# The tail of an attention and expert kernel: work after the attention ordered by a list scheduler

## What is computed

```
x = layernorm(x + attention(x))     # 16 heads of 16 channels, rotary, causal softmax; head i's scores get
                                    # cascade_w[i-1] * mean over the queries of head i-1's probabilities
x = layernorm(x + experts(x))       # 8 experts, each token goes to the one with the largest logit
    sel = argmax(x @ gate_w.T);  rw = sigmoid(max(x @ gate_w.T))
    xs = x * rw;  out = (xs @ w_up[sel].T * silu(xs @ w_gate[sel].T)) @ w_down[sel].T
layernorm(x) = (x - mean) / sqrt(var + 1e-5)
```

## Time and profile before

| | |
|---|---|
| median of three runs | 3644.92 us |
| lowest and highest | 3643.49, 3656.99 us |
| profiled execution: span | 3649.0 us |
| its busy shares: TensorE, VectorE, ScalarE, GpSimd | 86%, 72%, 85%, 55% |
| end of the attention (last attention instruction on VectorE) | 3398 us |
| routing's count, first gather of group 3, last scatter | 3486.0, 3518.2, 3645.4 us |

### The profile page before, as it was taken

The page is one execution under the profiler, slowest core; times in us unless marked ns, Lnnn a source line. Parts: engine busy times, 40 slices in busy tenths (PEclk is TensorE's granted clock), DMA queues, the critical chain, the costliest instruction groups (busy, mean ns, idle before and its releaser), DMA issues. The chain is left out here.

```text
span 3649.0 us, 92468 instructions
## 1 busy us (share of the span) xinstructions
PE 3133.0 (86%) x29690; PEld 1595.9 (44%) x29690; DVE 2612.1 (72%) x7930; ACT 3097.2 (85%) x8898; POOL 2009.9 (55%) x6184
## 2 busy tenths in 40 slices
PE   5788888888999889989998888899998888888855
PEld 3333333333444434444444443444444443344645
DVE  7566666666777777877877778787787767777666
ACT  3799999999998988988888999889888899988324
POOL 5555555554555356765665455675665633445345
PEclk8899999999999999999999999999999999999968
DMA  4332323333433443444444333435534432345354
GB/s 158 96 71 63 80 57 73 80 76 82 99 83 83 115 99 97 121 112 117 109 107 107 101 76 82 117 105 139 141 84 102 100 81 61 71 108 153 110 179 165
DMA packets 222519, 370.65 MB, mean 102 GB/s; under 512 B 49941, under 2 KB 165405, under 8 KB 209936
## 3 DMA queue, kind: packets, MB, share of 16 engines
q1 hardware_dynamic: 205968, 323.19, 35.9%
q0 software_dynamic: 14976, 37.34, 3.8%
q10 hardware_dynamic: 1088, 4.19, 0.3%
HBM read 259.76 MB, written 104.40 MB: 100 GB/s over the span
## 5 line engine op out<-in xcount | busy, mean ns | idle before, releaser
L1047 DVE CUSTOM_DVE_ANT_0 att_a<-scores,window 128x128 f32<-128x128 f32 (+7 forms) x2048 | 1508.6, 754 | 802.4 <-PE scores L720 654.4
L905 ACT ACTIVATE att_a<-att_a,neg_max 128x128 f32<-128x128 f32 (+7 forms) x2048 | 1598.0, 780 | 116.6 <-DVE neg_max L1047 112.9
L917 ACT ACTIVATE att_t<-scores 128x1024 f32<-128x1024 f32 (+7 forms) x2048 | 1334.6, 652 | 176.4 <-PE scores L739 163.5
L737 PE MATMUL scores<-q_stack,k_stack 104*128 104x512 bf16 (+3 forms) x3072 | 821.7, 335 | 328.6 <-ACT att_t L917 139.3
L755 PE MATMUL pv<-att_t,v_sb 128*32 128x256 f32 (+7 forms) x16384 | 828.7, 297 | 8.7 <-DVE o_sb L1081 8.2
L720 PE MATMUL scores<-k_stack,q_stack 99*128 99x512 bf16 (+3 forms) x3072 | 734.5, 334 | 28.1 <-DVE att_t L1094 10.1
L1389 POOL TENSOR_SCALAR guess<-row_sum 128x8 f32<-128x8 int32 x256 | 55.4, 216 | 1134.9 <-ACT att_a L905 1133.9
L755 PEld LDWEIGHTS pv<-att_t,v_sb 128*32 128x32 f32 x16384 | 376.5, 109 | 515.9 <-issue 428.3
L737 PEld LDWEIGHTS scores<-q_stack,k_stack 104*128 104x128 bf16 x3072 | 240.2, 98 | 735.4 <-DVE neg_max L1047 362.4
L739 PE MATMUL scores<-identb,mask 128*128 128x128 bf16 x2048 | 456.0, 223 | 0.0
L917 ACT ACTIVATION_READ_ACCUMULATOR att_t<-scores 128x1 f32 x2048 | 427.5, 209 | 0.0
(11 more groups left out here) (350 smaller groups left out, 4191.5 us busy)
## 6 DMA issues: line engine op xcount, KB each, us to landing
runner_r<-in_experts SPq DMA_DIRECT2D x137, 384.0 KB, 4.1
qk_parts<-of_proj SPq DMA_DIRECT2D x128, 384.0 KB, 2.6
q_stack<-qk_parts SPq DMA_DIRECT2D x378, 128.0 KB
k_stack<-qk_parts SPq DMA_DIRECT2D x378, 128.0 KB
of_proj<-in_xt SPq DMA_DIRECT2D x28, 1024.0 KB, 5.4
head_out<-o_sb SPq DMA_DIRECT2D x252, 64.0 KB
x_rows<-finisher_f SPq DMA_DIRECT2D x26, 514.0 KB, 4.7
finisher_f<-head_out SPq DMA_DIRECT2D x52, 256.0 KB, 5.1
```

What stands on the lines that cost most here:

```text
L737: engine.matmul(scores[:, c0:c1], ks[0:ROWS_B, j * P:(j + 1) * P], qs[0:ROWS_B, j * P + c0 - base:j * P + c1 - base], start=True, stop=True)
L905: engine.activation(taken, taken, EXP, scale=-1.0, bias=neg_max[:, n, i:i + 1], accum_out=row_sum[:, n, i:i + 1]).then_inc(s_exp_a, 1)
L917: engine.activation(att_t[:, ring:ring + end - base], scores[:, base:end], EXP, accum_out=col_sum[:, n, j:j + 1]).then_inc(s_exp_b, 1)
L1047: engine.tensor_tensor_reduce(out=att_a[:, ring:ring + end - base], in0=scores[:, base:end], in1=window[:, T - (end - base):T], op0=ALU.ad ...
```

## The change

All behind the attention, the steps are no longer made by `step(None, None)` but by a new function `by_readiness()`. It plays the tail on five engines with a table of durations, `EFFORT` (us of work, and us until a DMA's data have landed; all engines and all data free at time 0). Each time it looks for the stage with the earliest start, and on that stage's engine it takes, among the stages that could start within 0.2 us of it, first finishing and routing, then the lower group, then the earlier start. Each such stage becomes a step of its own. Second, group 3's batches get `t_root` on GpSimd and one Newton step on VectorE like all others. Third, `t_scale`, `t_turned` and `t_norm` are on ScalarE wherever they fall into the tail, not only in group 3 (`t >= TAIL` in place of `n[0] == GROUPS - 1`, with a wait in ScalarE for VectorE's last one before, `early`). `MIDWAY` only renames which stages carry on their job's bank. Nothing ahead of the tail changes.

```diff
     def norm_job(g, of):
-        root = [Stage("t_root", b, 2, phase=GPSIMD), Stage("t_newton", b, LAG)] if g < GROUPS - 1 else [Stage("t_newton", b, 1)]
-        return ([Stage("t_aggr", b, 0, after=tuple(("t_stat", (g, j), 1) for j in of))] + root + [Stage("t_norm", b, 1)]
+        return ([Stage("t_aggr", b, 0, after=tuple(("t_stat", (g, j), 1) for j in of)),
+                 Stage("t_root", b, 2, phase=GPSIMD), Stage("t_newton", b, LAG), Stage("t_norm", b, 1)]
...
+    BROUGHT = {"f_add": "f_x", "t_scale": "t_gather", "t_gu": "t_weights"}
+    HANDOVER = 0.1
+    PATIENCE = 0.2
+    EFFORT = dict(
+        f_load=Effort("SP", 0.2, 5.0), f_x=Effort("SP", 0.1, 5.0), f_pa=Effort("PE", 0.85), f_pb=Effort("PE", 0.85),
+        f_add=Effort("DVE", 1.5), f_aggr=Effort("DVE", 1.0), f_root=Effort("POOL", 1.0), f_newton=Effort("DVE", 0.9),
+        f_norm=Effort("ACT", 2.1), f_t=Effort("PE", 0.75), f_tm=Effort("ACT", 0.6),
...
+        t_gather=Effort("POOL", 1.0, 3.0), t_weights=Effort("SP", 0.4, 5.0), t_scale=Effort("ACT", 0.5),
+        t_turn=Effort("PE", 0.45), t_turned=Effort("ACT", 0.38), t_gu=Effort("PE", 1.1),
+        t_tanh=Effort("ACT", 0.3), t_gate=Effort("DVE", 0.28), t_up=Effort("DVE", 0.28), t_down=Effort("PE", 0.6),
+        t_add=Effort("DVE", 0.42), t_stat=Effort("DVE", 0.42), t_aggr=Effort("DVE", 0.8), t_root=Effort("POOL", 0.9),
+        t_newton=Effort("DVE", 0.9), t_norm=Effort("ACT", 0.6), t_out=Effort("POOL", 1.0, 3.0))
...
+            def rank(job):
+                s = job[0]
+                if s.kind[:2] in ("f_", "r_"):
+                    return 0
+                return s.key[0]
+            while active:
+                starts = [(earliest(job), n) for n, job in enumerate(active)]
+                starts = [(at, n) for at, n in starts if at is not None and at < float("inf")]
+                first, n = min(starts)
+                engine = EFFORT[active[n][0].kind].engine
+                _, at, n = min((rank(active[n]), at, n) for at, n in starts
+                               if at <= first + PATIENCE and EFFORT[active[n][0].kind].engine == engine)
...
-        while active:
-            step(None, None)
+        by_readiness()
...
-                    elif kind == "t_norm" and n[0] == GROUPS - 1:
+                    elif kind == "t_norm" and t >= TAIL:
+                        act.wait_ge(s["t_norm"], early["t_norm"])
...
                     elif kind == "t_newton":
-                        if n[0] < GROUPS - 1:
-                            dve.wait_ge(s["t_root"], nth["t_root", n])
-                            newton_step(norm_of(n), 1, s["t_newton"], False)
-                        else:
-
-                            y_ = norm_of(n).newton[:, 1, :].bitcast(I32)
-                            dve.wait_ge(s["t_aggr"], nth["t_aggr", n])
-                            dve.wait_ge(s_dve, chained(engine.tensor_scalar(y_, y_, -0.5, float(0x5f3759df), ALU.mult, ALU.add)))
-                            newton_step(norm_of(n), 3, s["t_newton"], True)
+                        dve.wait_ge(s["t_root"], nth["t_root", n])
+                        newton_step(norm_of(n), s["t_newton"], ("t_norm", n) in late)
```

More of the change, by code:

```diff
@@ L318, in step @@
                         banks[s.bank], used_by[s.bank] = t + 1, (s.kind, s.key)
-                    elif s.kind.endswith("_b") and id(job) in held_by:
-                        s.bank = held_by[id(job)]
-                    elif s.kind in ("f_pb", "r_sum", "t_tanh", "t_gate") and not s.hold:
+                    elif s.kind in MIDWAY and not s.hold and id(job) in held_by:
                         s.bank = held_by[id(job)]
@@ L419, in block_kernel @@
     steps, nth, total, PROLOGUE, TAIL = timetable()
+    late = {(st_.kind, st_.key) for step_ in steps[TAIL:] for st_ in step_.stages if st_.kind in ("t_scale", "t_turned", "t_norm")}
+    early = {kind: total[kind] - len([k for k, _ in late if k == kind]) for kind in ("t_scale", "t_turned", "t_norm")}
     TILE_OF = {(g, j): (j % RUN[g], j // RUN[g]) for g in range(GROUPS) for j in range(TILES)}
@@ L975, in scalar_program @@
                         made.then_inc(s["t_norm"], 1)
-                    elif kind == "t_turned" and n[0] == GROUPS - 1:
+                    elif kind == "t_turned" and t >= TAIL:
+                        act.wait_ge(s["t_turned"], early["t_turned"])
                         was = earlier(n)
@@ L981, in scalar_program @@
                         engine.copy(runner_of(n).xwT, room[:, 0:C]).then_inc(s["t_turned"], 1)
-                    elif kind == "t_scale" and n[0] == GROUPS - 1:
+                    elif kind == "t_scale" and t >= TAIL:
+                        act.wait_ge(s["t_scale"], early["t_scale"])
                         r, (b, _), was = runner_of(n), XS[n], earlier(n)
@@ L1009, in half, with newton_step @@
                 engine.tensor_scalar(norm.newton[:, 2, :], norm.moments[:, :, 1], EPS, -0.5, ALU.add, ALU.mult).then_inc(sem, 1)
-            def newton_step(norm, times, sem, shift):
+            def newton_step(norm, sem, shift):
                 a_, y_, h_ = (norm.newton[:, k, :] for k in range(3))
[L1014 to L1022, removed]
+                ev = chained(engine.tensor_tensor(a_, y_, y_, ALU.mult))
+                dve.wait_ge(s_dve, ev)
+                ev = chained(engine.tensor_tensor(a_, a_, h_, ALU.mult))
+                dve.wait_ge(s_dve, ev)
+                made = engine.scalar_tensor_tensor(out=norm.rstd, in0=a_, scalar=1.5, in1=y_, op0=ALU.add, op1=ALU.mult)
                 if shift:
+                    dve.wait_ge(s_dve, chained(made))
                     made = engine.scalar_tensor_tensor(out=a_, in0=norm.moments[:, :, 0], scalar=-1.0, in1=norm.rstd, op0=ALU.mult,
@@ L1351, in vector_program @@
                         chained(engine.bn_stats(norm_of(b).stats[:, b[1].index(n[1]), :], y_of(n)))
-                    elif kind == "t_norm" and n[0] < GROUPS - 1:
+                    elif kind == "t_norm" and t < TAIL:
                         norm = norm_of(n)
```

58 lines of the change are left out of this document (55 added, 3 removed).

## The result

The changed kernel takes 3633.24 us, median of six runs (3630.31 to 3635.83), beside 3648.32 us for the kernel before in the same session. The ratio is 0.9945 with a 95% interval of [0.993, 0.9959]: faster by 0.4 to 0.7%, about 20 us by the ratio, where 50 were forecast (3595 us, range 3574 to 3622). The two medians lie 15.1 us apart and the two profiled executions 20.5. The profiled execution took 3630.31 us with a span of 3628.5.

What follows compares the result with a forecast made beforehand. Step order was taken to bound finishing, VectorE's chain routing, and GpSimd then the rounds group 3's tiles, with GpSimd bounding them after the change. Savings of 34 + 7 + 9 = 50 us off 3644.9 gave 3595 us, range 3574 to 3622.

Steps and rivals of the forecast that it cites:

- A: Finishing, from 3400 us to `r_count`: bound by step order, 86 us to become 52, 34 us less.
- B: Routing, from `r_count` to group 3's first gather: VectorE's chain, 32.2 us to become 25, 7 less.
- C: Group 3's tiles, first gather to last scatter's end: GpSimd becomes the bound, 128.1 us to become 119, 9 less.
- 5.1 us, or 41 too: TensorE's price in finishing: 5.1 us a quad for projections, transposes and gates, 41 us for eight quads.
- What stands in GpSimd's queue of group 2: Group 2's leftover GpSimd work in group 3's stretch: an estimated four scatters, 5 us.
- an estimated 5 us of waiting: At the end, after GpSimd's last gather: waiting for a batch's aggregate, root, Newton step and norm, 5 us.
- The roots at their full 10 us: Group 3's ten roots moved to GpSimd, about 1.0 us each, would cost its tiles' stretch 10 us.
- TensorE's clock: Rival: thinly spread work keeps TensorE's clock low in group 3's tiles, 12 us longer there, 3616 us; chance 0.10.
- Waiting roots: Rival: roots stand before gathers in GpSimd's queue, group 3's tiles take 138 us, total 3614 us; chance 0.10.
- DMA at nothing: Changed order of SyncE's loads and stores in group 3's tiles costed at nothing, DMA share under 0.7.
- Group 2 last: Rival: group 2's tiles finish last, runners 0 to 3 start 25 us late, about half lost, 3622 us; chance 0.08.
- Slower: Rival: estimated durations misplace GpSimd's root and scatter groups, waits at each batch; at 8 us each 3665 us; chance 0.04.

Runs made afterwards that it cites:

- e5: Changed kernel with the scheduler's 40 durations replaced by measured ones; ratio to the kernel before 0.9934.
- e7: Changed kernel with one more four-column `pow` on GpSimd ahead of each of group 3's 39 gathers; ratio to the kernel before 1.0024.
- e9: Changed kernel without group 2's scatters behind group 3's first gather, their output rows not written; ratio to the kernel before 0.989.
- e2: Changed kernel with group 3's roots back on VectorE (guess and three Newton steps); ratio to the kernel before 0.9929.
- e1: Changed kernel with the old order of steps, keeping roots on GpSimd and the tail's stages on ScalarE; ratio to the kernel before 1.0001.
- e8: Changed kernel with measured durations, scheduler patience 0 in place of 0.2, and group 3's roots back on VectorE; ratio to the kernel before 0.9882.
- e11: Changed kernel with measured durations and scheduler patience 0 in place of 0.2, roots on GpSimd; ratio to the kernel before 0.9886.
- e3: Changed kernel with `t_scale`, `t_turned` and `t_norm` of group 2's tail tiles back on VectorE; ratio to the kernel before 0.9945.

## Why the prediction was wrong

The sign holds, and so does the mechanism in A and B and GpSimd as C's bound. The size doesn't: of the 41 us expected in A and B 31.2 came, and C, which was to give 9, took 11.0 back. By its steps:

**A, 34 us: the right cause, sized too high.** Quad after quad goes through, and ScalarE's norms are spread instead of standing in a block:

```profile
3419.13 2.08 ACT L1054 ACTIVATE finisher_f<-finisher_f 128x256 f32<-128x256 f32 x4 [4.74 <-DVE finisher_f L1112]
3423.07 2.07 ACT L1054 ACTIVATE of_proj<-of_proj 128x256 f32<-128x256 f32 x4
3429.35 2.08 ACT L1054 ACTIVATE of_proj<-of_proj 128x256 f32<-128x256 f32 x4 [1.53 <-DVE of_proj L1112]
...
3450.53 2.07 ACT L1054 ACTIVATE k_stack<-k_stack 128x256 f32<-128x256 f32 x4
```

`r_count` came 25.9 us earlier. The term that fell short is TensorE's: "5.1 us, or 41 too" for finishing and "4 for group 2's stages that get in". It was busy for 54.0 of A's 60 us. By line and in sum, finishing's matmuls show 47.3 us and those of group 2's tiles 13.3, 6.6 of them overlapping each other. The projection's price, 0.22 a record, was taken from one run at full speed; in A 112 of its 128 records (the others come ahead of 3400) took 28.4 us, 0.25 each, and transposes and gates 18.9 in place of 12.8. That TensorE sets A's length is shown by the executions of one order at two clocks above. The prediction costed the clock in A at nothing, though its own row had 0.85 there; between a clock of 0.90 and one of 0.95 it is 2.6 us. A sum of 60 was within the stated bounds of 43 and 65. Part of it is the plan: e5, with better durations, is 4.1 us earlier than e7.

**B, 7 us: right**, 5.3 measured. VectorE is busy for 25.1 of 28 us there, but for 46.1 of 60 in A, so the prediction's check, which let it be near full in both, holds for B alone. Routing's last result is there at 3484.1; the 3 us up to the gather are two scatters of group 2 on GpSimd.

**C, 9 us less: wrong by 20.** Two terms of it failed. "What stands in GpSimd's queue of group 2 (an estimated four scatters, 5 us)" was 20.0 us: 11 scatters, a gather, five roots. Four scatters came from no row. The earlier trace rows showed VectorE adding a tile of group 2 as late as 3502.75 even in the old order, and the change puts finishing and routing ahead of group 2 for all of A and B; four scatters were too few by the prediction's own reasoning. It named the place in B ("group 2's remaining tiles now fall here") and then did not carry their scatters into the stretch that it had just called bound by GpSimd. e7 shows that bound directly (38.1 us for 39.8), e9 the scatters' share in it (10.2 of 14.1 us). The second term, "an estimated 5 us of waiting" at the end, was 10.1: after its last gather GpSimd waits for ScalarE four times (2.61, 4.27, 2.86 and 1.58 us, of which 0.30 each are the usual gap), each time shortly behind a root whose Newton step and norm must come first. It has 25 scatters there and not some 20, but they are in the 98.7 all the same. 98.7 + 10.3 + 20.0 + 10.1 are C's 139.1. (The prediction's 108.9 for DMAs and roots should read 108.7; it changes nothing.)

**The roots at their full 10 us: right for this kernel, not as a rule.** C loses 8.4 us to them here (e2), 0.8 in the old order (e1) and 0.6 in the best (e8 and e11).

**The third part: no gain or loss that the runs can tell from nothing** (e3), but not by the working given: taking some 15 us off VectorE did not shorten A and B, which are shorter with the stages on VectorE, and that gain is paid back in late work.

**The signs.** `r_count` at 3460.1 lies 1.1 us outside 3452 ± 7, and the first gather at 3487.0 outside 3477 ± 8. Up to 3580 GpSimd is busy for over 0.75, as said; from 3580 to 3629 it is 0.59, and not only in the last 10 us.

**Rivals.** TensorE's clock did not fall in C as a whole; up to 3580 it was 0.90, where it had been 0.77 up to 3600, as the engine was busier (65.3 of 92 us against 56.7 of 82). Behind that it was 0.67, and whether this lengthens the last waits no run shows. The Trainium skill (TensorE: Matmul & The Clock Gate, A second HAM failure mode: psum-queue depth-cycling) tells of short idle times that make the clock swing. In C up to the last gather that can't have cost anything, as GpSimd never waits. In A, where the prediction did not look for it, the clock fell behind idle times of 0.78 and 1.27 us in one execution and not in another, and cost 2.6 to 4.8 us. Idle times alone, then, do not decide it here.

Waiting roots: no wait of over 3 us in the midst of C; the one of 4.27 and its three neighbours at the end are of this kind, 5 us more than the sum had for them. DMA at nothing: up to the last gather GpSimd waits for no data either, though the DMA share was 0.71 up to 3580, a little over the 0.7 that was said.

Group 2 last: the nearest in cause, and priced wrongly. With the plan's order laid beside the trace's gathers, runners 0 to 3 start group 3 at 3487.04, 3500.07, 3508.88 and 3528.19, runners 4 to 7 at 3488.34, 3506.38, 3507.63 and 3517.88. On average both sets start at about the same time (3506.0 and 3505.1). Only runner 3 trails, by 10.3 us behind the last of the others, because group 2's tile 35 is gathered there as late as 3503.88 and added at 3526.83. GpSimd issues without a pause all that time, so the loss went through its queue and not through runners that stood still.

Slower: it didn't come near. C at its own bound of 138 with A 8 us over its sum is 3595 + 19 + 8 = 3622, the range's end; C's 139.1 and B's 2 us put the tail's sum at 3625, just beyond it. The other 8 us up to 3633.24 are not the tail's: the forecast was taken off 3644.92, where the kernel before has a median of 3648.32 over six runs, and the changed kernel's profiled execution is its fastest, 2.9 us below its median.

## What to carry to other kernels

Work that a scheduler puts off is not hidden: it returns in the stretch whose bound it adds to, so count every instruction that the deferred work issues on that stretch's bounding engine. For a list scheduler, check where its own clock and the trace part: the plan as it stood gave 0.9945, correcting the durations or the tie rule alone 0.9934 and 0.9959, both together 0.9886. Before two orders are compared, look at the clock that each execution was granted: here it moved a keypoint by up to 4.8 us. And an engine's bound holds for one order: the same ten roots cost 8.4 us, 3.6 us or under 1 us, so measure such a part again after each change of order.

## What the runs showed of the hardware

An indirect DMA's issue behind a `pow` on GpSimd has a gap of 0.17 to 0.20 us ahead of it and behind another DMA one of 0.30; a `pow` of 1.05 us put between two of them costs 1.00 us (38.1 over 38, e7). With the same instructions and the same idle times of 0.78 and 1.27 us ahead, TensorE was granted 0.53 over 7 us in one execution and 1.00 in another; eight `t_gu` records took 1.75 us in the first and 1.13 in the second, four projection records 2.04 and 1.10. Ahead of the tail nothing was changed, and yet the attention's last instruction lay between 3393 and 3406 us in the fourteen profiled executions; keypoints of the tail compare only from there.
